# Fusing the update of a graph layer with the next layer's queries and keys, as tile pipelines

## The reference

```python
hidden = x @ Win.T + b_in                       # x is layer-normed here
for l in range(3):
    Q, K, V = (hidden @ W.T + b for each)       # 4 heads of 64
    scores = einsum('ehd,egd->ehg', Q[src], K[tgt]) / 8
    msg = einsum('ehg,egd->ehd', softmax(scores), V[tgt]) + Ee[et]
    m = segment_sum(msg @ Wo.T + bo, src)
    hidden = relu(layer_norm(hidden + m) * ln_g + ln_b)
g = x + (relu(hidden @ W1.T + b1) @ W2.T + b2)
x1 = x_in + g                                   # x_in: the raw input
out = x1 + experts(layer_norm(x1))              # softmax router, top 2 of 8
```

## Time and profile before

| | us |
|---|---|
| median of the three runs | 5030.3 |
| their lowest and highest | 5026.69, 5033.61 |
| the profiled execution | 4994.96 |
| its span, first to last instruction | 4992.9 |

### The profile page before, as it was taken

The page is one execution under the profiler, slowest core; times in us unless marked ns, Lnnn a source line. Parts: engine busy times, 40 slices in busy tenths (PEclk is TensorE's granted clock), DMA queues, the critical chain, the costliest instruction groups (busy, mean ns, idle before and its releaser), DMA issues.

```text
span 4992.9 us, 105216 instructions
## 1 busy us (share of the span) xinstructions
PE 3540.9 (71%) x32051; PEld 2742.5 (55%) x32052; DVE 2880.3 (58%) x7542; ACT 1974.2 (40%) x6195; POOL 2496.8 (50%) x2694
## 2 busy tenths in 40 slices
PE   4554066777777786777777777777777778629992
PEld 1113045666666644666666654566666665529991
DVE  7777025777677752777777764377777775620001
ACT  0000044444444445444444443544444444204440
POOL 4787705665666630566665642366666662041113
PEclk9998588999999968999999995899999996659996
DMA  1000034555555523555555542455555552515553
GB/s 27 1 1 6 16 106 128 158 159 156 156 161 160 158 64 131 150 158 159 158 159 159 156 127 87 137 158 160 161 159 160 161 157 82 173 68 185 184 179 111
DMA packets 258168, 640.75 MB, mean 128 GB/s; under 512 B 58336, under 2 KB 121325, under 8 KB 250286
## 3 DMA queue, kind: packets, MB, share of 16 engines
q0 software_dynamic: 161280, 480.04, 33.6%
q1 hardware_dynamic: 96830, 160.07, 9.5%
HBM read 589.52 MB, written 51.00 MB: 128 GB/s over the span
## 4 chain that ended last, share of the span: by engine, by line
PE 34%; DMA 21%; issue 18%; DVE 5%; POOL 4%; another core or an unknown queue 2%; SPq 1%; DVEq 1%; POOLq 1%; ACT 1%; ACTq 0%
DMA arena<-kv_d,gidx 19%; PE bank L1252 7%; PE bank L1242 5%; PE bank L1362 4%; PE bank L1229 4%; PE bank L1374 4%; PE bank L1219 3%; POOL arena L493 2%; PE bank L1235 1%; PE bank L1214 1%; DVE arena L750 1%; POOL tok_d L533 1%; DMA xin<-hid_d 1%; PE bank L1292 1%
## 5 line engine op out<-in xcount | busy, mean ns | idle before, releaser
L493 POOL DMA_INDIRECT arena<-kv_d,gidx x1776 | 1750.8, 986 | 1147.7 <-PE bank L1252 660.9
L1242 PEld LDWEIGHTS bank<-qbd,kt_s 128*128 128x128 f32 x7104 | 979.6, 200 | 55.3 <-ACT kt_s L994 26.4
L709 DVE TENSOR_REDUCE sc<-bank 128x32 f32<-128x512 f32 x888 | 613.7, 691 | 664.9 <-remote 363.4
L1242 PE MATMUL bank<-qbd,kt_s 128*128 128x128 f32 x7104 | 974.8, 282 | 26.7 <-ACT kt_s L994 24.4
L1229 PE MATMUL bank<-ident,arena 128*128 128x128 f32 x3552 | 696.8, 290 | 378.5 <-DMA arena<-kv_d,gidx 350.4
L1252 PE MATMUL bank<-att,arena 128*64 128x64 f32 x14208 | 654.0, 232 | 293.4 <-DVE arena L750 250.0
L1252 PEld LDWEIGHTS bank<-att,arena 128*64 128x64 f32 x14208 | 531.8, 140 | 472.7 <-issue 427.8
L994 ACT ACTIVATE kt_s<-bank 128x512 f32<-128x512 f32 x888 | 521.9, 588 | 581.2 <-PE bank L1229 548.9
L1229 PEld LDWEIGHTS bank<-ident,arena 128*128 128x128 f32 x3552 | 420.5, 145 | 539.6 <-DMA arena<-kv_d,gidx 511.9
L733 DVE TENSOR_TENSOR att<-at_s,arena 128x1024 f32<-128x1024 f32 x444 | 549.1, 1237 | 81.4 <-DVE at_s L730 74.6
L471 POOL DMA_INDIRECT rec_d<-arena x391 | 451.3, 1154 | 175.1 <-issue 126.9
(11 more groups left out here) (205 smaller groups left out, 3857.3 us busy)
## 6 DMA issues: line engine op xcount, KB each, us to landing
arena<-in_pack SPq DMA_DIRECT2D x56, 1030.0 KB, 5.1
arena<-kv_d,gidx POOLq DMA_INDIRECT x1776
xin<-hid_d SPq DMA_DIRECT2D x175, 128.0 KB
kv_d<-arena SPq DMA_DIRECT2D x75, 256.0 KB, 2.0
hid_d<-arena SPq DMA_DIRECT2D x100, 128.0 KB
arena<-in_w SPq DMA_DIRECT2D x4, 2048.0 KB, 9.5
y_d<-arena SPq DMA_DIRECT2D x56, 128.0 KB, 3.7
rec_d<-arena POOLq DMA_INDIRECT x391
```

The lines of the kernel that those rows point to most:

```text
L493: pool.indirect_dma_start(kv[:, t // UB, t % UB, :], None, kv_d, bass.IndirectOffsetOnAxis(gidx[:, h, t - h * HT:t - h * HT + 1], 0),).the ...
L709: dve.tensor_reduce(sc[:, p // 2 % 2, 2 * (p % 2):2 * (p % 2) + 2], bank[p % 4][:, :].rearrange("p (t g s h) -> p t g h s", t=2, g=H, s=W) ...
L1242: ins = mm(bk[:, o:o + P], kt_s[:, p % 2, u, c, :], qbd[:, p % 4, u, :], start=False, stop=(c == KC - 1), skip_group_check=True)
```

## The change

It does these things.

1. The update of layer l and the query stage of layer l+1 become one loop over steps (`uq_phase`), written out for all 25 tiles. In step k the engines update tile k, finish tile k-2, turn tile k-3, make queries and keys of tile k-4 and store those of tile k-5. The hidden tile is turned from where it was made, without the store and reload. The old hidden rows are still loaded for the sum.
2. The last update is fused with the final stage (`uf_phase`, steps up to k-10).
3. The turning of the sums moves from ScalarE to GpSimd (`turn_sums`, a ring of four). It becomes two plain copies since VectorE now adds the sums with the heads outside. The copy of the edge counts goes.
4. Gain and shift are folded into two passes, `(x - mean) * gain` and `x * (1/std) + shift`; the maximum with zero goes into ScalarE's copy of the turned tile, and for the next sum into VectorE's add.
5. GpSimd clears the sums after it has turned the last ones; for the first layer VectorE clears them, before it waits for the edge records.
6. Query weights are loaded at the start of `uq_phase`, update weights after the last update; the product of edge embeddings and `wo` moves to the end of the query part.
7. In the input stage ScalarE makes `xb`, which is x plus its normalised form, and SyncE stores it; the final stage loads it in place of raw x and doesn't normalise x. The second layer's bias comes in by a product with a row of ones. The second normalisation of the result becomes a second root with other constants, scaled on GpSimd.
8. The logits of all tiles go to one bank and the router's bias is added once. The expert weights come in eight loads of 1 MB as the sums are used up.
9. The loop over layers is written out on all engines.

The diff's core (ScalarE, VectorE and TensorE of `uf_phase` follow the same pattern as `uq_phase`, in more steps):

```diff
-            def store_h(i, base):
+            def store_x(i):
                 for j in range(G):
                     n = i * G + j
-                    hold(sp, S.hout_ready, base + n + 1)
+                    hold(sp, S.xb_ready, n + 1 + G)
+                    sp.dma_start(xb_d[rows(n), :], xb[:, j, :]).then_inc(rows_stored[j], 16)
+                    hold(sp, S.hout_ready, n + 1)
...
+                for k in range(NT + 5):
+                    if k + G < NT:
+                        sp.wait_ge(S.u_sum, at + k + 1)
+                        load_h(l, k + G)
+                    if k >= 5:
+                        n = k - 5
+                        sp.wait_ge(S.kvp_ready, hb + n + 3)
+                        sp.dma_start(kv_d[rows(n), :], kvout[:, n % G, :]).then_inc(kvo_stored[n % G], 16)
+                    if 2 <= k < NT + 2:
+                        n = k - 2
+                        sp.wait_ge(S.hout_ready, hb + n + 1)
+                        sp.dma_start(hid_d[rows(n), :], hout[:, n % G, :]).then_inc(h_stored[n % G], 16)
...
+            def turn_sums(l, n):
+                if n >= RA:
+                    pool.wait_ge(S.u_done, l * NT + n - RA + 1)
+                for r in range(2):
+                    pool.tensor_copy(
+                        aggT[r * DH:(r + 1) * DH, n % RA].rearrange("p c (w s) -> p c w s", s=W),
+                        acc[:, n * (P // W):(n + 1) * (P // W), :].rearrange("p w (c r s) -> p c w r s", c=KC, r=2)[:, :, :, r],
+                    ).then_inc(S.u_turned, 1)
+                    pool.wait_ge(S.u_turned, 2 * (l * NT + n) + r + 1)
+
+            def uq_phase(l):
+                pool.wait_ge(S.edges_all, l + 1)
+                for n in range(NT):
+                    turn_sums(l, n)
+                pool.memset(acc, 0.0).then_inc(S.sums_zeroed, 1)
+                pool.wait_ge(S.sums_zeroed, l + 2)
...
-                    dve.tensor_tensor(a, bank[6 + p % 2][u * DH:(u + 1) * DH, 0:DH], a, ALU.add).then_inc(S.chain_a if u == 0 else S.chain_b, 1)
+                    dve.tensor_tensor(a.rearrange("p (h s) -> p h s", h=H),
+                                      bank[6 + p % 2][u * DH:(u + 1) * DH, 0:DH].rearrange("p (s h) -> p h s", h=H),
+                                      a.rearrange("p (h s) -> p h s", h=H), ALU.add).then_inc(S.chain_a if u == 0 else S.chain_b, 1)
...
+                for k in range(NT + 5):
+                    if k < NT:
+                        summed(l, k)
+                    if 1 <= k <= NT:
+                        mean(l, k - 1)
+                    if k < NT:
+                        stats(l, k)
+                    if 1 <= k <= NT:
+                        scaled(l, k - 1)
+                    if 2 <= k <= NT + 1:
+                        inverse(l, k - 2)
+                    if k >= 5:
+                        n = k - 5
+                        dve.wait_ge(S.kvp_done, hb + n + 1)
+                        dve.wait_ge(kvo_stored[n % G], 16 + (l + 1) * NG * 16 + (n // G) * 16)
+                        dve.tensor_tensor(kvout[:, n % G, :], bank[6 + n % 2][:, :], bkv[:, :], ALU.add).then_inc(S.kvp_ready, 1)
+                    if 2 <= k <= NT + 1:
+                        shifted_out(l, k - 2)
+                edge_bias(l + 1)
...
+            edge_bias(0)
+            dve.memset(acc, 0.0).then_inc(S.sums_zeroed, 1)
             dve.wait_ge(S.rec_landed, 16)
...
+                for k in range(NT + 4):
+                    if 1 <= k <= NT:
+                        root(l, k - 1)
+                    if 3 <= k < NT + 3:
+                        hidden_out(l, k - 3, S.kvp_done)
+                    if k >= 4:
+                        n = k - 4
+                        act.wait_ge(S.q_done, (l + 1) * NT + n + 1)
+                        queries_out(n, bank[4 + n % 2], 0)
...
+                for k in range(NT + 4):
+                    if k < NT:
+                        update(l, k, 4)
+                    if 3 <= k < NT + 3:
+                        hidden_turned(l, k - 3)
+                    if k >= 4:
+                        n = k - 4
+                        if n == 0:
+                            pe.wait_ge(S.wl_landed, q_landed(l + 1))
+                        pe.wait_ge(S.hT_ready, hb + n + 1)
+                        if n >= 2:
+                            pe.wait_ge(S.q_ready, G + hb + n - 1)
+                        queries(bank[4 + n % 2], 0, n % G)
+                        if n >= 2:
+                            pe.wait_ge(S.kvp_ready, 2 + hb + n - 1)
+                        keys_values(bank[6 + n % 2], n % G)
```

More of the change, by code:

```diff
@@ L390, in _ @@
+            for l in range(L - 1):
+                uq_phase(l)
+            uf_phase(L - 1)
             sp.wait_ge(S.tok_blank, 1)
@@ new lines, in stats, with mean, scaled @@
+            def stats(l, n):
+                dve.wait_ge(S.u_sum, l * NT + n + 1)
+                dve.bn_stats(st[:, 0, n % G, :], x0[:, n % G, :]).then_inc(S.u_stat, 1)
+            def mean(l, n):
+                dve.wait_ge(S.u_stat, l * NT + n + 1)
+                dve.bn_aggr(mv[:, 0, n % G, :], st[:, 0, n % G, :]).then_inc(S.u_mean, 1)
+            def scaled(l, n):
+                j = n % G
+                dve.wait_ge(S.u_mean, l * NT + n + 1)
+                dve.scalar_tensor_tensor(out=x0[:, j, :], in0=x0[:, j, :], scalar=mv[:, 0, j, 0:1], in1=lng[:, :],
+                                         op0=ALU.subtract, op1=ALU.mult).then_inc(S.u_scaled, 1)
@@ new lines, in _ @@
+            bias(0)
+            for j in range(G):
+                dve.wait_ge(rows_stored[j], NG * 16)
+            with nc.vector.Fori(0, NG) as i:
+                for j in range(G):
+                    n = i * G + j
+                    hold(dve, S.kvp_done, n + 1)
+                    hold(dve, kvo_stored[j], (i + 1) * 16)
+                    dve.tensor_tensor(kvout[:, j, :], bank[5 + j % 3][:, :], bkv[:, :], ALU.add).then_inc(S.kvp_ready, 1)
+            edge_bias(0)
+            dve.memset(acc, 0.0).then_inc(S.sums_zeroed, 1)
@@ new lines, in _ @@
+            hold(act, S.bias_ready, 1)
+            with nc.scalar.Fori(0, NG) as i:
+                for j in range(G):
+                    hold(act, S.hT_done, i * G + j + 1 + G)
+                    act.activation(xT[:, j, :, :], bank[j][:, 0:D].rearrange("p (c n) -> p c n", n=P),
+                                   ACT.Copy).then_inc(S.hT_ready, 1)
+                for j in range(G):
+                    hold(act, S.q_done, i * G + j + 1)
+                    queries_out(i * G + j, bank[j], D)
@@ L1223, in e_phase, with edge_bias @@
+            def edge_bias(l):
+                pe.wait_ge(S.wl_landed, u_landed(l))
+                for c in range(KC):
+                    ins = mm(bank[0][0:TYPES, 0:D], eeT[:, c, :], wo[:, c, :], start=(c == 0), stop=(c == KC - 1))
+                ins.then_inc(S.ee_done, 1)
+                pe.wait_ge(S.ee_ready, l + 1)
             def e_phase(l):
@@ new lines, in _ @@
+            hold(pe, S.wl_landed, u_landed(0))
+            with nc.tensor.Fori(0, NG) as i:
+                for j in range(G):
+                    n = i * G + j
+                    pe.wait_ge(rows_landed[j], (NG + i + 1) * 16)
+                    pe.wait_ge(S.q_ready, n + 1)
+                    for c in range(KC):
+                        ins = pe.transpose(bank[j][:, c * P:(c + 1) * P], xin[:, j, c * P:(c + 1) * P], ident[:, :])
+                    ins.then_inc(S.hT_done, 1)
+                for j in range(G):
+                    n = i * G + j
+                    pe.wait_ge(S.hT_ready, n + 1)
+                    queries(bank[j], D, j)
+                    pe.wait_ge(S.kvp_ready, n + 1)
+                    keys_values(bank[5 + j % 3], j)
@@ L1296, in _ @@
+            hold(pe, S.q_ready, NT + G)
+            edge_bias(0)
             pe.wait_ge(S.onehot_ready, 4)
```

663 lines of the change are left out of this document (356 added, 307 removed).

## The result

The changed kernel takes 4902.12 us (median of four runs, 4889.53 to 4910.84) beside 5031.95 for the kernel before in the same comparison: ratio 0.974, interval 0.9721 to 0.976, 130 us less. The forecast was 4805 with a range of 4750 to 4885. The sign was right, the size wrong: 225 us were to be saved. The profiled execution took 4901.8 us, its span 4900.0.

The account below looks back on a forecast made before the run. Edge phases are the bulk, barely touched; the seams' update is a chain by groups that can run under the queries. Savings 148 + 91 - 9 - 5 = 225 us off the 5030.3 us median give 4805 us, range 4750 to 4885.

Parts of the forecast that it names:

- The seams: Last edge sum to first gather between layers: 124.8 us each, 74.2 less than now, 148 us over two.
- The clearing beside VectorE: In each seam, GpSimd's clearing of the sums holds up a VectorE pass: 6 us, bounds 0 and 10.8.
- The last part: Last update fused with final stage: thirty-five steps make 134.5 us against 225.3, saving 91 us.
- the fourth rival: Whole kernel: nothing overlaps, the four queues wait in turn, about the present time; chance 0.02.
- The full step of the last part: TensorE's products per tile there: 4.95 us, taken as 5.1 because of the clock.
- The low clock: Fused steps: TensorE stays at the low clock, 8.1 us per seam step, 8.5 in the last part, 5054 us; chance 0.06.
- VectorE as the bound: Fused steps: VectorE, slowed by GpSimd's copies, paces at 5.2 us for 4.15, 6.2 for 5.1, 4879 us; chance 0.25.
- Roots on ScalarE: Update's roots in fused steps: 0.30 us each, no table load counted; two loads per tile would give 5.3 us.
- Input stage and first edge phase: Before the first scores: +9 us for new input-stage work, +5 us for the first clearing on VectorE.
- The +5 for the clearing: First edge phase: clearing on VectorE delays one-hots some 9 us, gathers start 11 us sooner; between 0 and +9.
- The strided add and the written-out layers: Edge phases: adds reading PSUM with step four priced at nothing, bounds 0 and +40 us; written-out loops counted nothing.
- The anchor: Whole kernel: the 225 us come off the runs' median, 5030.3 us, 35 us above the profiled execution.

Follow-up runs that it names:

- e4: The kernel before with only the edge sums' heads outside (strided VectorE add), on the faster sort of chip: 4416.10 us, ratio 1.0.
- e9: The kernel before itself, unchanged, one run on the faster sort of chip: 4411.69 us.
- e11: The kernel before with heads outside and layers written out, on the faster sort of chip: 4403.44 us, ratio 0.9976 to before.
- e12: The kernel before with heads outside and layers written out, on the slower sort of chip: 5035.00 us, ratio 1.0014 to before.
- e7: The changed kernel with z's turn later in TensorE's last-part step and the first clearing on GpSimd after the scatter: 4823.12 us, ratio 0.9592 to before.
- e1: The changed kernel with z's turn moved behind the first-layer product in TensorE's last-part step, faster sort of chip: 4191.07 us, ratio 0.9485 to before.
- e10: The changed kernel with three unread products ahead of both waits before z's turn, faster sort of chip: 4221.44 us, ratio 0.9558 to before.

## Why the prediction was right or wrong

- **The seams** were right: 124.8 us expected, 128.3 and 127.8 measured, 139 us gained instead of 148. Part of that is luck, since terms inside cancelled.

```profile
1830.11 1.91 PE L1354 MATMUL bank<-xT,wq 128*128 128x128 f32 x8
...
1871.75 0.69 PE L1433 MATMUL bank<-eewo,arena 4*128 4x256 f32 x2
...
1876.21 0.69 PE L1433 MATMUL bank<-eewo,arena 4*128 4x256 f32 x2
```

  Queries start 1830.11 - 1811.5 = 18.6 us after the last sum, not 12.3: five updates precede them on TensorE, not three. The full step is 1876.21 - 1871.75 = 4.46 us, not 4.15, mostly because the update's third product has four partitions and takes 0.62 us where I had put two records of 0.216: "An update is three products, six records, 1.30 us". The other way, the clearing cost 0, not 6.
- **The clearing beside VectorE** ran from 1904.78 to 1915.54. VectorE's passes in it are as long as elsewhere, and start on time:

```profile
1904.78 10.76 POOL L570 MEMSET arena<- 64x12800 f32 x1
```

```profile
1908.23 0.42 DVE L862 TENSOR_TENSOR arena<-bank,xin 128x256 f32<-128x256 f32 x1 [2.14 <-PE bank L1433]
...
1910.08 0.47 DVE L893 SCALAR_TENSOR_TENSOR arena<-arena,rs,lnb 128x256 f32<-128x256 f32 x1
```

  The late pass in the earlier trace rows was held by the clearing all the same. Its line, L683, normally takes 0.41 us. In both clearings between layers of before, e4, e9, e11 and e12, the one L683 that begins inside the clearing takes 2.60 to 3.28 us and ends 0.15 us after it, ten times out of ten. Of the five in before's second clearing (shortest, median, longest in ns):

```profile
L683 DVE TENSOR_SCALAR arena<-arena,mv,rs x5: 395/400/3003, 3059.3 to 3063.2; 128x256 f32<-128x256 f32 x5
```

  What was wrong here is "VectorE's new passes are SBUF to SBUF with a column scalar, as that one was": L683 reads one tensor from SBUF, L878 and L893 read two, and none of the passes of these two lines is late. The Trainium skill, SBUF — State Buffer, section "SBUF: two separate sides", by which a VectorE pass with two SBUF inputs is held up only by a GpSimd operation that reads SBUF, agrees with this trace.
- **The last part** was wrong by 83 us: 134.5 expected, 217.3 measured. The step that failed is the sentence under the fourth rival: "I see no circular wait in the orders, each step asks for results one to three steps old." A result one step old is no distance at all when it is made at the end of that step and asked for at the start of the next. `z` was such a result. In the forecast's terms: fifteen full steps 131 us instead of 76.5, ten draining 40 instead of 25, ten filling 46 instead of 33. In e7, without the loop, they are 76.5, 23 and 42: the loop and its clock cost some 73 us of the 83, and the filling, priced at 3.3 us a step, was some 9 us too short by itself.
- **The full step of the last part** came out right, 5.1 us forecast and 5.10 in e1 and e7, but that is luck in part. In e7's step the update takes 1.66 us for 1.30, the turn 0.37 for 0.25 and the second layer with its bias row 1.59 for 1.30; the logits take 0.37 for 0.85 and the first layer 0.89 for 1.0.
- **The low clock,** my second rival with 8.5 us for the full step there, came true in this place alone (8.74 us), but not for the reason I gave, a clock that doesn't rise after a slow update stage: it had risen, to 1.00, and a wait brought it down.
- **VectorE as the bound** did not happen: between its passes it waits 2.14 us per step in the seam and 6.65 in the last part. The pairing that this rival feared does show, on the other engine: a GpSimd copy of the sums (L560) that begins inside a VectorE pass with two SBUF inputs takes 0.53 to 0.66 us instead of 0.40 and ends 0.26 us after the pass, 15 times out of 15 in the changed kernel. The pass keeps its 0.47 us, and GpSimd has room.
- **Roots on ScalarE** bring no table load per tile, as said (one at the first root of each of these stages): they take 0.30 us each (L1174), and the idle time ahead of them is a wait for VectorE.
- **Input stage and first edge phase**: 14 us expected, 5.0 measured at the first scores. The +5 for the clearing has no cause left, as e7 shows. The input stage's last add came at 681.9 instead of 678.5, 3.4 us later, not 9; in e12, with the input stage of before, it came at 681.2 and the scores later still, so not even these few microseconds are shown to be the change's.
- **The strided add and the written-out layers** were priced at nothing, with up to 40 us kept as a bound; on chip A they cost some 14 together (9 to 18).
- **The anchor** was right: I took the saving off the median, not off the profiled execution. The sum over medians is 139.4 + 8.0 - 5.0 - 14 = 128 us, or 133 if the 5 are among the 14; 130 measured.

## What to carry to other kernels

Before a software pipeline is priced, walk once around it: for each wait, ask where in the producer's step the result is made and where in the consumer's step it is asked for, and add up what stands between in both orders. A result one step old can close a loop, and here one moved block (e1) gave back 73 us. Judge a short wait on TensorE by what the clock does afterwards: here 1.1 us of wait took 2.5 us more with it.

## What the runs showed of the hardware that was not expected

- Waits of only 1.1 us, once in every step, made TensorE's clock go up and down (0.50 from 4122 to 4126 us, 0.82 from 4134 to 4138, 0.72 on average) while it was busy for 87% of the time. Useless products in the gap brought it back to 1.00 (e10). The Trainium skill, TensorE: Matmul & The Clock Gate, section "A second HAM failure mode: psum-queue depth-cycling", tells of a clock that goes back and forth where the engine pauses briefly and often between groups of products; this trace agrees.
- Products over few partitions are slow for their size: two records of 256 columns over four partitions take 4115.36 - 4114.73 = 0.63 us at the full clock, those over 128 partitions 0.96/2 = 0.48.
- Two sorts of chip differ by 14% in the kernel before, with seams and last part alike: 155 against 183 GB/s in the edge phase at clocks of 0.98 and 0.99 (e12, e9), and an input stage that ends at 532 (e9) or at 681 us (e12) while the scatter ends at 627 in both.
- GpSimd's clearing held a VectorE pass that reads one tensor from SBUF and writes one as large back (L683) to its own end, ten times out of ten; passes that read two (0.47 us), that read PSUM (0.42) or that write only statistics (0.43) kept their length beside it.
- GpSimd's issues of gathers took 2.2 to 2.4 us each while VectorE made the one-hots, 0.95 beside VectorE's clearing just before. In e7, where the one-hots start ahead of the first gather, its first three take 2.2 to 2.3 us and the next 0.95. From the changed kernel:

```profile
780.72 0.94 POOL L537 DMA_INDIRECT arena<-kv_d,gidx  x1 [0.30 <-issue]
...
783.32 2.43 POOL L537 DMA_INDIRECT arena<-kv_d,gidx  x1 [0.30 <-issue]
```

```profile
771.54 10.72 DVE L970 MEMSET arena<- 64x12800 f32 x1 [2.72 <-issue]
782.29 10.23 DVE L976 TENSOR_TENSOR arena<-iotab,rec 128x2368 bf16<-128x2368 bf16 x4
```
